# A key-value attention in which the second attention's scores move into two blocks of row-half matmuls, and its later steps move on by one

## The reference

```
h = h + _L0_ffn_ref(_layernorm(h, axis=-1), Wq_pk, pk_keys, Wq, keys_table, values_table, Wo)

q = (x @ Wq).reshape(b, n, HEADS, DIM) * DIM ** (-0.5)        # HEADS 8, DIM 64
kv_scores, indices = _pk(x, Wq_pk, pk_keys)                    # the 16 best of 64 x 64 keys, per token and head
k = einsum('bnhk,bnhkd->bnhd', kv_scores, keys_table[ind])
v = einsum('bnhk,bnhkd->bnhd', kv_scores, values_table[ind])
sim = einsum('bihd,bjhd->bhij', q, k)                          # causal, then softmax
out = einsum('bhij,bjhd->bhid', softmax(sim), v)
return out.reshape(b, n, HEADS * DIM) @ Wo
```

## Time and profile before

| | |
|---|---|
| median of 3 runs | 1962.24 us (1961.16 to 1962.26) |
| the profiled execution | 1959.13 us, span 1957.3 us |
| busy share of the span | PE 97%, PEld 75%, DVE 82%, ACT 75%, POOL 67% |
| mean granted clock of TensorE | 0.991 |
| the loop | PE from about 229 us to about 1940 us |

### The profile page before, as it was taken

The page is one execution under the profiler, slowest core; times in us unless marked ns, Lnnn a source line. Parts: engine busy times, 40 slices in busy tenths (PEclk is TensorE's granted clock), DMA queues, the critical chain, the costliest instruction groups (busy, mean ns, idle before and its releaser), DMA issues.

```text
span 1957.3 us, 43650 instructions
## 1 busy us (share of the span) xinstructions
PE 1898.5 (97%) x11464; PEld 1470.7 (75%) x11464; DVE 1607.9 (82%) x4824; ACT 1466.0 (75%) x2969; POOL 1313.8 (67%) x1575
## 2 busy tenths in 40 slices
PE   5997899999999999999999999999999999999997
PEld 3765577777777777777777777777777777777776
DVE  3646788888888888888888888888888888888886
ACT  3763477887877787877877777777877777877775
POOL 1112377777777777777777777777777777777775
PEclk9998999999999999999999999999999999999999
DMA  3001100001000200020000100020001100020001
GB/s 108 2 1 47 57 22 20 20 20 61 14 20 20 64 18 16 17 64 20 20 20 16 57 20 20 20 62 16 17 20 38 47 19 16 14 64 20 20 18 28
DMA packets 118094, 58.00 MB, mean 30 GB/s; under 512 B 109696, under 2 KB 116032, under 8 KB 116733
## 3 DMA queue, kind: packets, MB, share of 16 engines
q1 hardware_dynamic: 115250, 56.75, 11.1%
q10 hardware_dynamic: 2795, 0.70, 0.2%
HBM read 24.55 MB, written 0.70 MB: 13 GB/s over the span
## 4 chain that ended last, share of the span: by engine, by line
PE 76%; issue 7%; POOL 6%; DVE 1%; ACT 0%; POOLq 0%; DMA 0%; SPq 0%; DVEq 0%; ACTq 0%
PE ps L978 26%; PE ps L986 14%; PE ps L969 13%; PE ps L990 7%; PE ps L1028 4%; POOL k_W_low L1374 3%; PE ps L1046 3%; PE ps L963 2%; PE ps L1038 2%; PE ps L1013 2%; PE ps L1000 1%; PE ps L1006 1%; POOL k_aS L1316 0%; PE ps L1029 0%; POOL k_cand L1330 0%
## 5 line engine op out<-in xcount | busy, mean ns | idle before, releaser
L1540 DVE SCALAR_TENSOR_TENSOR k_W<-ps,k_W 128x688 f32<-128x688 f32 x1028 | 892.6, 868 | 230.5 <-ACT k_W L1184 211.1
L1374 POOL TENSOR_TENSOR k_W_low<-k_W,k_W_high 128x688 fp32r<-128x688 f32 x513 | 850.5, 1658 | 337.9 <-ACT k_W_high L1189 337.9
L1184 ACT ACTIVATE k_W<-ps 128x688 f32<-128x688 f32 x1029 | 765.7, 744 | 364.0 <-PE ps L969 354.1
L978 PE MATMUL ps<-k_W,k_tab 128*128 128x344 f32 x2048 | 676.5, 453 | 0.0
L969 PE MATMUL ps<-k_X,sel 128*128 128x344 f16 x2058 | 471.3, 310 | 8.1 <-DVE k_W L1540 7.4
L978 PEld LDWEIGHTS ps<-k_W,k_tab 128*128 128x128 f32 x2048 | 366.1, 190 | 127.5 <-issue 0.5
L1189 ACT ACTIVATE k_W_high<-k_W 128x688 fp32r<-128x688 f32 x513 | 395.6, 771 | 0.0
L986 PE MATMUL ps<-k_W_high,k_tab_high 128*128 128x344 f32 x1024 | 385.6, 379 | 0.0
L986 PE MATMUL ps<-k_W_high,k_tab_low 128*128 128x344 f32 x1024 | 324.6, 320 | 0.0
L969 PEld LDWEIGHTS ps<-k_X,sel 128*128 128x128 f16 x2058 | 176.3, 99 | 177.9 <-issue 79.1
L990 PE MATMUL ps<-k_W_low,k_tab_high 128*128 128x344 f32 x1024 | 244.3, 319 | 0.0
(11 more groups left out here) (233 smaller groups left out, 2313.0 us busy)
## 6 DMA issues: line engine op xcount, KB each, us to landing
k_tab<-in_tables SPq DMA_DIRECT2D x9, 2048.0 KB, 7.3
k_X<-k_spl SPq DMA_TRANSPOSE x390, 2.4
k_xs<-x2T SPq DMA_DIRECT2D x33, 172.0 KB, 2.2
k_qT<-k_qs SPq DMA_DIRECT2D x33, 86.0 KB, 2.0
cst<-in_consts SPq DMA_DIRECT2D x1, 1024.0 KB, 20.6
wts<-in_weights SPq DMA_DIRECT2D x1, 896.0 KB, 12.9
cst<-in_consts SPq DMA_DIRECT2D x1, 874.5 KB, 17.3
xr<-in_xrows SPq DMA_DIRECT2D x1, 750.0 KB
```

The costliest lines, as they stand in the source:

```text
L978: mm = mm_(sums, tab[:, slot, at + k, :], W[:, d % RING, k, :], start=(d == 0 and k == 0), stop=(d == NDC - 1 and k == 1))
L1184: A(W[:, d % RING, :, :], ps[:, 2 * (d % 2):2 * (d % 2) + 2, 0:LOUT], ACT.Exp).then_inc(e_done, 1)
L1374: G.tensor_tensor(W_low[:, q % SPLIT_RING, :, :], W[:, d % RING, :, :], W_high[:, q % SPLIT_RING, :, :].bitcast(F32), ALU.subtract).then_i ...
L1540: V.scalar_tensor_tensor(W[:, d % RING, :, :], ps[:, 2 * (d % 2):2 * (d % 2) + 2, 0:LOUT], 0.0, W[:, d % RING, :, :], ALU.is_ge, ALU.mult) ...
```

## The change

Three things are changed at once.

1. The fp32 matmuls of value projection, keys and similarities use 64 rows of the array. Projections and similarities take rows 0 to 63 (`wos[0:64]`, `kv[0:64]`, `xs`, now 64 rows by two batches), keys take rows 64 to 127 (`qT[64:128]`, `kv[64:128]`). The mask comes first, over the whole width of a tile (`causb` is widened by 256 columns of zeros), with all rows.
2. They stand in two blocks. At d = 7 `first_scores` has the masks of tiles 0 and 1, their keys, and the three projections; at d = 8 `last_scores` has the mask and keys of tile 2 and the three similarities. At d = 5 and d = 6 PE keeps only `queries`.
3. The steps behind move on by one: on PE `turn_probabilities` to d = 12, `attention_output` to d = 14; on ACT the copy of the similarities to d = 9, the copy of the projected values and the probabilities to d = 10, the copy of the turned probabilities to d = 13; on DVE `row_max` and all of `halves_*`, `row_sum` and so on by one or two. The wait for `vw_ready` moves from the scores to `turn_probabilities`, and that for `kv_ready` into `first_scores`. SP issues the transposes before `xs`, which is now two transfers.

```
-                def attention_scores(i, pj, pairs):
+                def project_values(t, head):
+                    t0, m = TT[t]
+                    bank, c0 = value_area(t)
+                    rhs = wos[0:64, head, :] if isinstance(head, int) else wos[0:64, bass.ds(head, 1), :].rearrange("p a d -> p (a d)")
+                    return mm_(ps[0:m, bank, c0:c0 + 64], kv[0:64, t0:t0 + m], rhs, start=True, stop=True)
+
+                def causal_mask(t, pj):
+                    t0, m = TT[t]
+                    bank, c0 = score_area(t, pj)
+                    mm_(ps[0:m, bank, c0:c0 + t0 + m], eyeb[0:m, 0:m], causb[0:m, 256 - t0:256 + m], start=(t != 1), stop=False)
+
+                def key_scores(t, pj):
+                    t0, m = TT[t]
+                    bank, c0 = score_area(t, pj)
+                    return mm_(ps[0:m, bank, c0:c0 + t0 + m], qT[64:128, pj, t0:t0 + m], kv[64:128, 0:t0 + m], start=False, stop=(t > 0))
+
+                def similarities(t, par, head):
+                    t0, m = TT[t]
+                    return mm_(ps[0:m, MID0, 128 * t:128 * t + 128], xs[:, par, t0:t0 + m],
+                               wf[0:64, 0, bass.ds(head, 1), :, :].rearrange("p a b k -> p (a b) k"), start=True, stop=True)
+
+                def first_scores(i, pj, pairs, head):
...
-                    wait_alone(pe, vw_ready, i + 1)
...
+                    wait_alone(pe, kv_ready, i + 1)
+                    for t in range(2):
+                        causal_mask(t, pj)
+                    key_scores(0, pj)
+                    project_values(2, head).then_inc(last_mm, 1)
+                    key_scores(1, pj)
+                    project_values(0, head)
+                    project_values(1, head).then_inc(vw_mm, 1)
+
+                def last_scores(i, pj, pairs, following=None):
+                    if following is not None:
+                        pe.wait_ge(sim_ready, i + 2)
+                        wait_alone(pe, xs_ready, pairs * 32 + 32)
+                    causal_mask(2, pj)
+                    pe.wait_ge(last_mm, i + 1)
+                    key_scores(2, pj).then_inc(s_mm, 1)
+                    if following is not None:
+                        for t in range(NT):
+                            mm = similarities(t, *following)
+                        mm.then_inc(sim_mm, 1)
...
@@ (PE, the loop)
                             if d == 5:
                                 if par == 0:
                                     queries(i, slot, pair, nj)
-                                project_values(i, g // 4 if par else ((g + 31) // 4) % 8)
-                            if d == 6:
-                                similarities(i + 2, par, (g + 1) // 4, g)
                             if d == 7:
-                                attention_scores(i, nj, g)
-                            if d == 11:
+                                first_scores(i, nj, g, g // 4 if par else ((g + 31) // 4) % 8)
+                            if d == 8:
+                                last_scores(i, nj, g, (par, (g + 1) // 4))
+                            if d == 12:
                                 turn_probabilities(i, nj)
-                            if d == 13:
+                            if d == 14:
                                 attention_output(i)
...
@@ (ACT)
                 def copy_projected_values(i):
                     act.wait_ge(vw_mm, i + 1)
+                    act.wait_ge(nmax_done, i * 3 + 3)
...
-                                copy_projected_values(i)
-                            if d == 7:
-                                copy_similarities(i + 2)
-                            if d == 9:
+                            if d == 9:
+                                copy_similarities(i + 2)
+                            if d == 10:
+                                copy_projected_values(i)
                                 for t in range(NT):
                                     probabilities(i, nj, t)
-                            if d == 12:
+                            if d == 13:
                                 copy_turned_probabilities(i)
...
@@ (DVE)
-                            if d == 9:
+                            if d == 10:
                                 row_max(i, nj)
...
-                            if d == 8:
+                            if d == 10:
                                 halves_max(i + 2, False)
-                            if d == 10:
+                            if d == 11:
                                 halves_drop(i + 2, 0)
                                 softmax_sum(i + 1)
-                            if d == 11:
+                            if d == 12:
                                 halves_drop(i + 2, 1)
                                 row_sum(i)
```

More of the change, by code:

```diff
@@ L236, in _ @@
                 nc.gpsimd.tensor_copy(eyeb[:, :], const("eye")).then_inc(cast_done, 1)
-                nc.gpsimd.tensor_copy(causb[:, :], const("causal")).then_inc(cast_done, 1)
+                nc.gpsimd.memset(causb[:, 0:256], 0.0).then_inc(cast_done, 1)
+                nc.gpsimd.tensor_copy(causb[:, 256:384], const("causal")).then_inc(cast_done, 1)
             @block.tensor
@@ L833, in _ @@
                 sync.wait_ge(ln_done, NPAIR + 2)
-                sync.dma_start(xs[:, :], x2T[:, 1, :]).then_inc(xs_ready, 16)
+                for par in range(2):
+                    sync.dma_start(xs[:, par, :], x2T[64 * par:64 * par + 64, 1, :]).then_inc(xs_ready, 16)
                 sync.wait_ge(zeroed, 9)
@@ L858, in item @@
                     def item(i, slot, par, g, pair):
+                        turn_scores(i + 1, 1 - par)
                         if par == 1:
                             wait_alone(sync, sim_mm, i + 3)
-                            sync.dma_start(xs[:, :], x2T[:, bass.ds((pair + 2) % NPAIR, 1), :].rearrange("p a s -> p (a s)")).then_inc(xs_ready, 16)
-                        turn_scores(i + 1, 1 - par)
+                            for b in range(2):
+                                sync.dma_start(xs[:, b, :], x2T[64 * b:64 * b + 64, bass.ds((pair + 2) % NPAIR, 1), :].rearrange("p a s -> p (a s)")).then_inc(xs_ready, 16)
                         if par == 0:
@@ L953, in _, with first_similarities @@
                 mix(2)
[L956 to L959, removed]
+                def first_similarities(n):
                     for t, (t0, m) in enumerate(TT):
-                        rhs = wf[:, par, head, :, :] if isinstance(head, int) else \
-                            wf[:, par, bass.ds(head, 1), :, :].rearrange("p a b k -> p (a b) k")
-                        mm = mm_(ps[0:m, sim_bank(n), 128 * t:128 * t + 128], (x2T[:, 0, :] if g is None else xs)[:, t0:t0 + m], rhs, start=True, stop=True)
+                        mm = mm_(ps[0:m, sim_bank(n), 128 * t:128 * t + 128], x2T[:, 0, t0:t0 + m], wf[:, n, 0, :, :], start=True, stop=True)
                     mm.then_inc(sim_mm, 1)
@@ L1007, in queries @@
                         start=True, stop=True).then_inc(q_mm, 1)
[L1009 to L1013, removed]
-                    mm.then_inc(vw_mm, 1)
-                def attention_scores(i, pj, pairs):
+                def project_values(t, head):
[16 more added lines that the diff above has]
+                def first_scores(i, pj, pairs, head):
                     if pj == 0:
@@ L1055, in keep_busy @@
                         mm_(ps[:, 3, 0:LOUT], const("mean"), x2T[:, 0, :], start=True, stop=True)
-                similarities(0, 0, 0)
+                first_similarities(0)
                 mix(3)
@@ L1060, in _ @@
                 pe.wait_ge(ret_done, 3)
-                similarities(1, 1, 0)
+                first_similarities(1)
                 keep_busy(3)
@@ L1125, in _ @@
                 spread_gains(n, 1)
-                project_values(n, H - 1)
-                attention_scores(n, 1, H * NPAIR)
+                first_scores(n, 1, H * NPAIR, H - 1)
+                last_scores(n, 1, H * NPAIR)
                 turn_probabilities(n, 1)
```

27 lines of the change are left out of this document (12 added, 15 removed).

## The result

| | before | after |
|---|---|---|
| median of 4 runs | 1961.91 us | 1985.29 us (1984.26 to 1986.97) |
| the profiled execution | 1959.13 us | 1986.97 us |
| mean granted clock of TensorE | 0.991 | 0.988 |

The change makes the kernel slower by 1.2%: the ratio is 1.0121, with a 95% interval of 1.0103 to 1.0138. The forecast was 1986 us.

What follows compares the result with a forecast made beforehand. PE bounds the kernel. Blocks -0.34, waits +0.65 and even wait +0.12 give +0.31 an odd and +0.43 an even item; 32 pairs add 23.7 to 1959.1, 1982.8, and 3.1 for the median: 1986 us, range 1943 to 2016.

Steps and rivals of the forecast that it cites:

- Saving of the blocks: PE's two blocks take 1.17 and 1.16 us, 2.33 for 2.67 before: 0.34 us an item less.
- 0.35 for both changes of the array's shape: Each PE block goes into row halves and back; the two changes together are taken to cost 0.35 us.
- rival 4: PE's halves overlap less, similarities and projections starting late if matmuls keep program order: 31 us more, 2017 us; chance 0.13.
- The chain behind d = 10: ACT reaches the next item's chunk 0' late, so PE waits 0.44 and 0.21 us, together 0.65 an item.
- The 64 x 2 waits: Expected sign: PE's waits on DVE, some 64 x 2 entries of 0.44 and 0.2 us, before d = 13 and d = 14.
- ends a us later, before chunk 14 comes: DVE's `row_max`, before d = 10, is done before chunk 14 comes at 1.33, so the copy's wait for it costs nothing.
- The even item's wait: Even items' first block on PE waits for ACT's queries' copy: 0.45 us where it was 0.33, 0.12 more.
- ACT is not late: Rival: chunk 0' reaches PE by 4.71, so the item keeps -0.34: 1940 us, down to 1930; chance 0.14.
- the two cancel: Rival: wait and saving cancel, with shape changes at 0.1 each or only the first wait: 1955 to 1968 us; chance 0.10.
- No overlap: Rival: the row halves in each PE block do not overlap at all: 72 us more, 2058 us; chance 0.03.
- More waits: Rival: more waits than those worked out: 2005 us and up; chance 0.04.
- The sum: Odd item +0.31 us, even item +0.43, over 32 pairs +23.7 us: 1982.8 profiled, 1986 median.

Runs made afterwards that it cites:

- Run 4: Changed kernel with projections, keys and similarities on all 128 rows again (other half multiplied by zeros), same placement and order: 2024.4 us.
- Run 1: Changed kernel with ACT's three probabilities behind the exponential of chunk 0' (d = 11) and the table's high part in d = 12: 1957.6 us.
- Run 6: Changed kernel with ACT's copy of the projected values in d = 9 and not d = 10: 1973.0 us.
- Run 5: Kernel before the change with only the later steps moved on by one, without the blocks: 1990.2 us.
- Run 2: Changed kernel with ACT's copy of the queries in d = 6 ahead of the high part of the split weights: 1972.7 us.
- run 8: 1944.1 us kernel (probabilities after chunk 0', queries' copy first, values' copy in d=9), with split scores' high part ahead of everything in d=6: 2011.7 us.

## Why the prediction was right

**Saving of the blocks**, predicted -0.34 an item from 1.17 and 1.16: measured 1.19 and 1.12, -0.36. Taking 0.35 for both changes of the array's shape held as a part of the sum; no run measures it by itself. Run 4 adds what the prediction did not tell apart: the halves give 0.52, and the wider masks take back 0.16.

**Matmuls in program order** (rival 4, 2017 us) fell: keys and similarities start together, at 1033.55, though a second pass of the keys stands between them. In the Trainium skill ("TensorE: Matmul & The Clock Gate", section "Step-by-step: what each phase is for") matmuls stay in program order; the trace does not agree across row halves, as the retention had suggested.

**The chain behind d = 10**, predicted: ACT at chunk 0' 3.47 after the start of d = 10, d = 13 at 5.15, a wait of 0.44 and one of 0.21. Measured 3.44, 5.16, 0.45 and 0.18. Run 1 shows the mechanism by taking the probabilities away from there: d = 13 loses its wait and d = 12 all but 0.15. That 0.15 was hidden behind the larger wait. The 64 x 2 waits that the prediction named as its sign are there on the weight loads. Run 6 shows the share of the copy, 0.18. Run 5 shows that the move of the later steps costs as much without the blocks, but by another way, `row_max` ahead of chunk 14. I had held that `row_max` "ends a us later, before chunk 14 comes" and costs nothing; that is so only with the blocks.

**The even item's wait**, predicted 0.45 where it was 0.33: measured 0.41. Run 2 shows that the order on ACT alone makes it.

**The other rivals.** For "ACT is not late" (2) the wait would have had to be under 0.3 an item, and it is 0.63. For "the two cancel" (3) either the blocks had to take about 2.0 or the second wait had to be absent; the blocks take 2.31, and both waits are there. "No overlap" (5) falls with rival 4. "More waits" (6) gave too high a time, but waits that the prediction does not have did come, at the restarts of the loop.

**The sum**, predicted +0.31 odd and +0.43 even: measured +0.27 and +0.36, which is 32 x 0.63 = 20 us, not 23.7. The loop was 24.9 longer. What the sum lacked are three items of 64, those in which the outer loop starts its body again: their step d = 0 takes 4.15, 3.87 and 3.75 us after the change, and 3.07, 3.06 and 3.03 before. With the first item of the loop, they lie 12.3 us above the other even items. Before it was 7.1, and 0.8 more for one other item: +4.4. After the first of these waits the granted clock falls (windows of after, then of before):

```profile
669.00:672.00 3.00, 3.00 (x14) 2.66 (x15) 3.00 (x14) 0.88 (x2) 1.13 (x3) 0.65 0.99 419
```

```profile
661.30:665.00 3.70, 3.70 (x22) 3.04 (x23) 3.70 (x15) 2.35 (x4) 2.32 (x6) 1.00 1.03 436
```

DVE stands idle for 3.5 us there for no reason that the trace shows ("issue"):

```profile
DVE k_W L1571 <- issue: 9.7, 3, 3.5
```

The kernel before has no such entry. Run 5 has it (9.5 us in 3 waits, and d = 0 at 3.82, 3.95 and 3.77), so the move of the later steps brings it without the blocks. What DVE waits for is open. So the total came within a microsecond partly by luck: 3.5 us too much in the items stood against 4.4 that were not foreseen. In the profiled execution, forecast at 1982.8 and measured at 1987.0, 1.2 of the 4.2 us lie in the loop and 3.0 ahead of it.

## What to carry to other kernels

In a pipeline written by hand, a step moved on by one is an edit on every engine's queue: count from its new neighbours when the next piece of the main loop comes through, on ACT and DVE as well as on PE. Here PE's own work fell by 0.36 us an item, and two pieces of ACT's work in the wrong place, the probabilities and the queries' copy, turned that into a loss of 1.2%; with both elsewhere the same blocks gave 0.9%. Where several small instructions of DVE stand beside a busy POOL, as the three comparisons do here, try to make them one.

## What the runs showed of the hardware

- Matmuls on rows 0 to 63 and on rows 64 to 127 run at once, and a group of one half starts ahead of an earlier pass of the other (1033.55 and 1033.91). They save 0.52 us of 2.83. If the shorter group of each block were hidden in full it would be 0.55 + 0.58 = 1.13, so by this estimate a block in halves pays 0.3 us for being in halves.
- Three DVE comparisons that take 0.26 us alone took 1.46, 1.14 and 1.67 while POOL ran without a gap: each ended 0.06 to 0.07 us behind one of POOL's instructions. The Trainium skill ("SBUF — State Buffer", section "Who interferes with whom") says that DVE's `tensor_scalar` can enter modes that take a pair of ports shared with GpSimd; whoever issues first holds the pair for the whole instruction, and the other is blocked fully. The trace agrees, and adds that the price is paid for each instruction anew.
- A wait of 1.9 us on PE was followed by a granted clock of 0.50 in 9 of 32 items of run 8, and not in the other 23; the wait of 0.28 us that the trace shows before d = 13 after the change left the clock at 1.00 (mean over the loop).
